# Expert results scattered to their tokens' rows, and plain loads in place of gathers

## What is computed

```python
xt = x.reshape(T, Dd)                      # T = 2048 tokens
scores = softmax(xt @ Wr.T)                # 8 experts
k_scores, k_ids = top_k(scores, 2)
k_w = k_scores / (k_scores.sum(-1) + eps)
h = relu(xt @ Wg[e].T) * (xt @ Wu[e].T)    # 512 wide
out_e = h @ Wd[e].T
out = sum over the two chosen e of k_w[e] * out_e
```

## Time and profile before

| | |
|---|---|
| median of 3 runs | 1273.29 us (1267.78 to 1274.67) |
| profiled execution | 1278.91 us, of it the span 1277.1 us |
| PE busy | 87% of the span |
| DVE, ACT, POOL busy | 71%, 63%, 44% |
| last eviction of an expert tile | 1249.10 us |

### The profile page before, as it was taken

One profiled execution on the slowest core, in us unless ns is written; L12 is line 12 of the kernel. 1 busy time (PEld: TensorE's weight loads), 2 busy tenths in 40 slices (PEclk: granted clock), 3 DMA queues, 4 the chain that ended last, 5 costly groups with the idle time before them and its releaser, 6 DMA issues.

```text
span 1277.1 us, 36892 instructions
## 1 busy us (share of the span) xinstructions
PE 1109.0 (87%) x14528; PEld 798.7 (63%) x14528; DVE 902.2 (71%) x1818; ACT 808.4 (63%) x1488; POOL 564.4 (44%) x1193
## 2 busy tenths in 40 slices
PE   5667899999999999999989989986879878798990
PEld 1123576776677676667767767775545445698990
DVE  4757689997899998899976787784457567152231
ACT  5786788887998897897876676663334333232430
POOL 1004366666566666666755664654010103104404
PEclk9989799999999999999998999998699888898995
DMA  4012262222222212222213222311001103398982
GB/s 151 1 49 69 49 164 54 56 72 53 51 65 55 58 45 78 53 54 72 54 45 83 62 54 71 66 37 30 10 14 22 28 9 125 112 295 285 335 292 54
DMA packets 131661, 106.33 MB, mean 83 GB/s; under 512 B 60112, under 2 KB 119376, under 8 KB 131232
## 3 DMA queue, kind: packets, MB, share of 16 engines
q1 hardware_dynamic: 129440, 99.76, 27.8%
q0 software_dynamic: 2048, 4.20, 1.0%
HBM read 84.06 MB, written 15.73 MB: 78 GB/s over the span
## 4 chain that ended last, share of the span: by engine, by line
PE 50%; DVE 24%; issue 10%; ACT 6%; POOL 5%; DMA 3%; SPq 2%; DVEq 0%; POOLq 0%; ACTq 0%
PE bank L1051 6%; PE pair L731 5%; DVE vc L1500 4%; DVE kc L1500 4%; PE bank L1058 3%; PE pair L695 3%; PE bank L1005 3%; DVE AM L1570 3%; PE bank L878 2%; PE bank L833 2%; PE bank L783 2%; POOL xs L1997 2%; DVE X L1654 2%; PE pair L849 2%; PE bank L772 2%
## 5 line engine op out<-in xcount | busy, mean ns | idle before, releaser
L1954 POOL TENSOR_TENSOR SU<-SU 128x14 f32<-128x14 f32 (+6 forms) x448 | 151.1, 337 | 35.1
L1950 POOL TENSOR_TENSOR SU<-SU 128x14 f32<-128x14 f32 (+6 forms) x448 | 149.6, 334 | 34.9
L1500 DVE SCALAR_TENSOR_TENSOR vc<-vy,conv,vc 128x512 f32<-128x512 f32 x192 | 152.8, 796 | 16.8 <-ACT vc L1193 16.4
L1500 DVE SCALAR_TENSOR_TENSOR kc<-ky,conv,kc 128x512 f32<-128x512 f32 x162 | 125.7, 797 | 10.0 <-ACT kc L1167 8.3
L2020 POOL TENSOR_TENSOR RR<-RR,nh 128x8 f32<-128x8 f32 x32 | 65.1, 2036 | 150.0 <-DVE RR L1642 149.9
L1836 DVE TENSOR_TENSOR vy<-bank,vc 128x512 f32<-128x512 f32 x46 | 31.8, 692 | 98.5 <-PE bank L1051 97.2
L731 PE MATMUL pair<-SM,KQ 64*128 64x128 f32 (+1 forms) x512 | 75.0, 370 | 20.3 <-DVE AM L1570 14.1
L1926 POOL TENSOR_TENSOR st<-st,nh 128x4 f32<-128x4 f32 x16 | 18.9, 1180 | 148.1 <-DVE st L1476 110.3
L695 PE MATMUL pair<-xnT,WQ 128*128 128x512 f32 x128 | 76.6, 682 | 0.2 <-DVE SM L1519 0.2
L663 PE MATMUL pair<-xnT,WQ 128*128 128x512 f32 x128 | 70.3, 634 | 5.9 <-ACT qb L1167 5.1
L1799 DVE TENSOR_REDUCE SM<-pair 128x4 f32<-128x1024 f32 x32 | 39.1, 1222 | 40.4 <-PE pair L963 40.3
(11 more groups left out here) (316 smaller groups left out, 3154.9 us busy)
## 6 DMA issues: line engine op xcount, KB each, us to landing
AM<-in_wex_dram SPq DMA_DIRECT2D x32, 768.0 KB, 5.6
SM<-dscr SPq DMA_DIRECT2D x58, 256.0 KB, 3.8
V<-in_wex_dram SPq DMA_DIRECT2D x14, 768.0 KB, 5.1
et<-dscr SPq DMA_DIRECT2D x38, 256.0 KB, 3.8
SM<-fscr SPq DMA_DIRECT2D x64, 128.0 KB, 2.9
scratch<-AM SPq DMA_DIRECT2D x128, 48.0 KB, 1.8
SU<-scratch SPq DMA_DIRECT2D x256, 15.5 KB
xs<-idle SPq DMA_DIRECT2D x2, 1472.0 KB, 9.4
```

Source lines behind the costliest of these rows:

```text
L1500: e.scalar_tensor_tensor(c, y[:, :, k:k + 256], conv[:, ct, k:k + 1], c, ALU.mult, ALU.add).then_inc(s_c, 1)
L1950: e.tensor_tensor(tmp[:, 0:k, 0:15 - k], sub[:, 0:k, k:k + 1].to_broadcast([128, k, 15 - k]), sub[:, k:k + 1, k + 1:16].to_broadcast([128, ...
L1954: e.tensor_tensor(sub[:, 0:k, k + 1:16], sub[:, 0:k, k + 1:16], tmp[:, 0:k, 0:15 - k], ALU.subtract).then_inc(s_su, 1)
```

## The change

Results no longer come back by gathers. Each sorted row now carries where its result belongs, and the results are scattered there from SBUF.

- A row of `xs` has 130 columns. Column 128 is the token's number in its half (128 h + partition), written by DVE into the normed tokens from the constant `place`; column 129 is 0 for choice 0 and 1024 for choice 1, written by a memset on POOL. So POOL scatters all eight token tiles for k = 0, waits until these have landed, sets column 129, and scatters them again for k = 1. Rows that no token fills keep 2048 and up, so that their results go to rows which nobody reads.
- `clear()` fills `xs` with these numbers and zeroes, now from a DRAM input instead of SBUF, in rows of 520 bytes.
- `place` (DVE), in each tile's tick: the sum of the two columns as an integer, into one of six index buffers.
- `back` (POOL) replaces `store`: an indirect DMA with that index writes the tile's results to `ys[S]`, now (16 + 23) x 128 rows. In the ticks in which POOL sends the scatters of half 1, the results of tiles 13 to 19 are put off to ticks 70 and 73. `YB` has six buffers instead of three, the loads six places instead of eight, and a load also waits for `place` of the tile six before it.
- `res` is on SP: per half four plain loads, two for each four token tiles (one per choice).

```diff
@@ scratch and buffers
-        xs_d = [nc.dram_tensor(f"xs{i}", (NS * 128, 128), F32, kind="Internal").ap() for i in range(2)]
-        ys_d = [nc.dram_tensor(f"ys{i}", (NS * 128, 128), F32, kind="Internal").ap() for i in range(2)]
+        xs_d = [nc.dram_tensor(f"xs{i}", (NS * 128, 130), F32, kind="Internal").ap() for i in range(2)]
+        ys_d = [nc.dram_tensor(f"ys{i}", ((16 + NS) * 128, 128), F32, kind="Internal").ap() for i in range(2)]
...
-        XSR = [kcf[:, 128 * k:128 * k + 128] for k in range(NX)]
+        XSR = [kcf[:, 130 * k:130 * k + 130] for k in range(NX)]
+        place = kyf[:, 880:888]
+        IDX = [PPf2[:, k:k + 1] for k in range(NX)]
...
-        YB = [YFf[:, 640 + 128 * k:768 + 128 * k] for k in range(3)]
+        YB = [YFf[:, 640 + 128 * k:768 + 128 * k] for k in range(3)] + [SU[:, 128 * k:128 * k + 128] for k in range(3)]
+        NY = len(YB)
@@ ticks
-            for h in range(8):
-                t = b + 5 + (2 * h // 3 if S else h)
-                at_tick(t, ("scat", S, h, t))
+            for m in range(16):
+                t = b + 5 + m // (3 if S else 2)
+                at_tick(t, ("scat", S, m, t))
...
-            at_tick(TILE[i] + 1, ("store", i))
+            at_tick(TILE[i], ("place", i))
+            at_tick({67: 70, 68: 73, 69: 73, 70: 73, 71: 73, 72: 73}.get(TILE[i] + 1, TILE[i] + 1), ("back", i))
...
-            b = TB[1] + 3 + 2 * t if t < 8 else TILE[-1] + 2 + t - 8
-            at_tick(b, ("res", t))
+            b = TB[1] + 3 + 2 * t if t < 8 else TILE[-1] + 2
+            if t % 4 == 0:
+                at_tick(b, ("res", t // 4))
@@ SP
             def clear():
-                e.wait_ge(s_set, NS_SET - 1)
-                z = idle[:, 0:256].bitcast(F32)
                 for S in range(2):
-                    e.dma_start(xs_d[S].rearrange("(i p) c -> p i c", p=128), z.unsqueeze(1).to_broadcast([128, NS, 128])).then_inc(l_zero, 16)
+                    e.dma_start(xs_d[S].rearrange("(i p) c -> p i c", p=128),
+                                lay2_d[:, LAY2 + 8:].rearrange("p (i c) -> p i c", i=NS)).then_inc(l_zero, 16)
...
                     if i >= NX:
                         e.wait_ge(s_et, i - NX + 1)
+                        e.wait_ge(s_place, i - NX + 1)
...
-                elif kind == "store":
-                    i, = a
-                    e.wait_ge(s_ye, i + 1)
-                    e.dma_start(ys_d[i // NS][128 * (i % NS):128 * (i % NS) + 128, :], YB[i % 3]).then_inc(l_ys[i % 3], 16)
+                elif kind == "res":
+                    u, = a
+                    S, half = u // 2, u % 2
+                    for k in range(NY):
+                        e.wait_ge(l_ys[k], 16 * len([i for i in range(NS * (S + 1)) if i % NY == k]))
+                    if S:
+                        e.wait_ge(s_xo, 8 * half + 8)
+                    for k in range(2):
+                        r = 1024 * k + 512 * half
+                        e.dma_start(GB[half][:, :, k, :], ys_d[S][r:r + 512, :].rearrange("(t p) n -> p t n", p=128)).then_inc(l_g[half], 16)
@@ ACT, eviction of Y
-                    if i >= 3:
-                        e.wait_ge(l_ys[i % 3], 16 * (i // 3))
-                    e.activation(YB[i % 3], bank[7][:, 0:128], ACT.Copy).then_inc(s_ye, 1)
+                    if i >= NY:
+                        e.wait_ge(l_ys[i % NY], 16 * (i // NY))
+                    e.activation(YB[i % NY], bank[7][:, 0:128], ACT.Copy).then_inc(s_ye, 1)
@@ DVE
+                elif kind == "place":
+                    i, = a
+                    e.wait_ge(l_xs[i % NX], 16 * (i // NX) + 16)
+                    if i >= NX:
+                        e.wait_ge(l_ys[(i - NX) % NY], 16 * ((i - NX) // NY) + 16)
+                    e.tensor_scalar(IDX[i % NX], XSR[i % NX][:, 128:129], XSR[i % NX][:, 129:130], None, ALU.add).then_inc(s_place, 1)
@@ POOL
                     if h == 0:
-                        e.wait_ge(l_zero, 32)
-                    for k in range(2):
-                        e.indirect_dma_start(xs_d[S], bass.IndirectOffsetOnAxis(ap=POS[S][:, k, h:h + 1], axis=0), XE[S][:, h, :],
-                                             None).then_inc(l_sc[S], 16)
-                elif kind == "res":
...
+                        if k == 0:
+                            e.wait_ge(l_zero, 32)
+                        else:
+                            e.wait_ge(l_sc[S], 128)
+                        e.memset(XE[S][:, :, 129], 1024.0 * k).then_inc(s_one, 1)
+                        e.wait_ge(s_one, 2 * S + k + 4)
+                    e.indirect_dma_start(xs_d[S], bass.IndirectOffsetOnAxis(ap=POS[S][:, k, h:h + 1], axis=0), XE[S][:, h, :],
+                                         None).then_inc(l_sc[S], 16)
+                elif kind == "back":
+                    i, = a
+                    e.wait_ge(s_ye, i + 1)
+                    e.wait_ge(s_place, i + 1)
+                    e.indirect_dma_start(ys_d[i // NS], bass.IndirectOffsetOnAxis(ap=IDX[i % NX], axis=0), YB[i % NY], None).then_inc(
+                        l_ys[i % NY], 16)
```

More of the change, by code:

```diff
@@ L25 @@
 LAY2 = 624
-NX = 8
+NX = 6
 def flat(a):
@@ L99, in program @@
         vy = sb("vy", [128, 2, 2, 259])
-        kc = sb("kc", [128, 2, 512])
+        KC = sb("kc", [128, 1040])
+        kc = KC[:, 0:1024].rearrange("p (a t) -> p a t", a=2)
         vc = sb("vc", [128, 2, 512])
-        et = sb("et", [128, 2, 512])
-        qb = sb("qb", [128, 2, 512])
+        ET = sb("et", [128, 1040])
+        et = ET[:, 0:1024].rearrange("p (a t) -> p a t", a=2)
+        QB = sb("qb", [128, 1040])
+        qb = QB[:, 0:1024].rearrange("p (a t) -> p a t", a=2)
         xT = sb("xnT", [128, 3, 512])
@@ L142, in program @@
         CT = [Uf[:, 512 * i + 256:512 * i + 512] for i in range(2)]
+        PPf2 = flat(PP[:, :, :])[:, 376:376 + NX].bitcast(U32)
         XE = [a.rearrange("p (t n) -> p t n", t=8) for a in (etf, qbf)]
-        XSR = [kcf[:, 128 * k:128 * k + 128] for k in range(NX)]
+        XSR = [kcf[:, 130 * k:130 * k + 130] for k in range(NX)]
+        place = kyf[:, 880:888]
+        IDX = [PPf2[:, k:k + 1] for k in range(NX)]
         XST = [YFf[:, 384 + 128 * k:512 + 128 * k] for k in range(2)]
-        YB = [YFf[:, 640 + 128 * k:768 + 128 * k] for k in range(3)]
+        YB = [YFf[:, 640 + 128 * k:768 + 128 * k] for k in range(3)] + [SU[:, 128 * k:128 * k + 128] for k in range(3)]
+        NY = len(YB)
         RG = [vcf[:, 512 * k:512 * k + 512] for k in range(2)]
         HB = [vyf[:, 512 * k:512 * k + 512] for k in range(2)]
-        GB = [[Vf[:, 3072 + 256 * i + 128 * k:3072 + 256 * i + 128 * k + 128] for k in range(2)] for i in range(4)]
+        GB = [a.rearrange("p (t k n) -> p t k n", t=4, k=2) for a in (Vf[:, 3072:4096], AMf[:, 8192:9216])]
         WR = [AMf[:, 1536 * k:1536 * k + 1536] for k in range(4)] + [Vf[:, 1536 * k:1536 * k + 1536] for k in range(2)]
@@ L207, in program @@
         l_sc, l_xs, l_w, l_ys, l_g = (sem("l_sc0"), sem("l_sc1")), [sem(f"l_xs{k}") for k in range(NX)], [sem(f"l_w{k}") for k in range(6)], [
-            sem(f"l_ys{k}") for k in range(3)], [sem(f"l_g{k}") for k in range(4)]
+            sem(f"l_ys{k}") for k in range(6)], [sem(f"l_g{k}") for k in range(2)]
+        s_place = sem("s_place")
         s_et, s_xt, s_g, s_u, s_rg, s_h, s_y, s_ye, s_xo = (sem(f"s_{n}") for n in ("et", "xt", "g", "u", "rg", "h", "y", "ye", "xo"))
@@ L927, in prep @@
                 if kind == "Q":
-                    e.wait_ge(l_aw, 16)
+                    e.wait_ge(l_aw, 32)
                     e.wait_ge(s_nxT, NI["at", q] + 1)
@@ L1042, in expert @@
                     e.wait_ge(*free(("T", i)))
-                    e.transpose(bank[7][:, 0:128], XSR[i % NX], ident[:, :]).then_inc(s_et, 1)
+                    e.transpose(bank[7][:, 0:128], XSR[i % NX][:, 0:128], ident[:, :]).then_inc(s_et, 1)
                 elif kind in ("G", "U"):
@@ L1820, in item @@
                     norm2(*a)
+                    key = a[0]
+                    if key[0] == "ex" and key[1] % 2 == 0:
+                        e.tensor_copy(XE[key[1] // 2][:, :, 128], place)
+                elif kind == "place":
[4 more added lines that the diff above has]
+                    e.tensor_scalar(IDX[i % NX], XSR[i % NX][:, 128:129], XSR[i % NX][:, 129:130], None, ALU.add).then_inc(s_place, 1)
                 elif kind == "signed":
@@ L1987, in item @@
                 elif kind == "scat":
-                    S, h, t = a
+                    S, m, t = a
+                    h, k = m % 8, m // 8
                     e.wait_ge(s_ix2, 2 * S + 1)
@@ L1994, in item @@
                     if h == 0:
-                        e.wait_ge(l_zero, 32)
-                    for k in range(2):
-                        e.indirect_dma_start(xs_d[S], bass.IndirectOffsetOnAxis(ap=POS[S][:, k, h:h + 1], axis=0), XE[S][:, h, :],
-                                             None).then_inc(l_sc[S], 16)
-                elif kind == "res":
```

(13 more changed lines are left out.)

17 lines of the change are left out of this document (9 added, 8 removed).

## The result

| | before | changed |
|---|---|---|
| median of 20 runs each, us | 1276.07 (1267.78 to 1281.38) | 1280.05 (1273.39 to 1288.09) |
| ratio, with its 95% interval | | 1.0036 [1.0019, 1.0054] |
| profiled execution (its span), us | 1278.9 (1277.1) | 1285.7 (1283.9) |

The changed kernel is slower by 0.36%: a small loss, but a real one, where the sum had said a small gain. The two profiled executions lie 6.8 us apart in span. To say where they went, I read the same marks in both traces: DVE's transposes of SU in round 1 and round 5, the first scatter and T(0) of half 0, the first scatter and T(23) of half 1, the last eviction, and the end.

What follows compares the result with a forecast made beforehand. PE was taken as full during expert tiles and idle before each half's first tile and in the tail; -10.1 (tail) + 5.4 (half 1) + 0.6 (half 0) + 3.0 (clearing) = -1.1 us, giving 1272.2 against 1273.3, range 1264.5 to 1281.

Steps and rivals of the forecast that it cites:

- The clearing: Early stage, SP's queue: clearing xs from DRAM in 520 B rows loses 3 us, passed on through POOL and ACT to PE.
- Upper end: Clearing of xs: each byte costs twice, 3.06 MB at 141 GB/s instead of 283, 10.9 us more.
- the lower end: Clearing of xs: it moves at the same rate as before, loss 0.
- My hope against it: Early stage: ACT also waits 3.2 us for PE in the same round, so part of a slower clearing may be caught up.
- The prediction's own sign of being wrong: Early stage: the forecast is wrong if it loses over 6 us or nothing.
- The slower rival: SP's queue, 159 to 185 us: clearing at half its rate delays ACT's exponentials, 10.9 instead of 3, total 1280.1; chance 0.20.
- The tail: After the last tile: one scatter, plain loads and eight additions replace 16 gathers, gain 10.1 us.
- my better end: Tail after the last tile: scatter landing in 2.5 us and loads in 3.2 give a gain of 12.1.
- Half 1's start: POOL's scatters before T(23): the wait for choice 0 and one result scatter make T(23) 5.4 us late.
- The second queue: Half 1's start: evictions of tiles 19 and 20 wait for delayed result scatters, end just ahead of T(23)'s load, cost nothing.
- Half 0's start: Before T(0): the wait for choice 0 falls into a hole on POOL; two memsets and some landing lose 0.6 us.
- Result buffers as a limit: Half 1, rival: result scatters landing in 8 us or more hold PE after T(23); at 9 us +3, 1275.2; chance 0.07.

Runs made afterwards that it cites:

- A: The kind of chip on which the kernel before took 1275 us; on the other kind it took 1306 to 1307.
- two groups of scatters: Changed kernel with choice 0's scatters in two groups of four, each with its own semaphore and memset: 0.9945 of before's time, on chips where before took 1306 to 1307.
- the contiguous clearing: Changed kernel with xs cleared from DRAM as one contiguous stretch of 11,960 B per partition instead of 23 rows of 520 B: 0.9932 of before's time, median 1267.42 us.

## Why the prediction was wrong

The forecast was 1272.2, a gain of 1.1 us on either base; measured were 1280.05, a loss of 4.0 between medians and 6.8 between profiles. The time lies inside the range of 1264.5 to 1281, at its upper end, and the ratio inside 0.5%, but on the other side of 1.

- **The clearing: the step that failed.** "Upper end: each byte costs twice" and "I stay near the lower end and take 3". Measured: 15.0 in the first trace, 13.9 and 14.0 in two others of the changed kernel on A; the landing 12.3 us longer. Two faults. I put the question to the wrong feature: DRAM as a source costs nothing (9.4 us), rows of 520 B do (+12.4 alone), and the earlier trace rows could speak only of rows that start on multiples of 512 B in xs. And the bound wasn't a bound: it priced the clearing's own bytes, not what the loads behind it on SP's queue lose. The decay rows came 13.7 us late, not 10.9; the rest of the 15.0, 1.3 us, is what is left for PE's restart at the granted clock of 0.50 shown above. My hope against it, that ACT's 3.2 us wait for PE would catch a part, didn't come true: PE had run out of work too and stood idle from 179 to 187 us, and the same wait is still there in the changed kernel, 3.11 us long. The prediction's own sign of being wrong, an early stage that loses over 6 us, is what came.
- **The page that spoke against me was right that the rows cost.** The Trainium skill, DMA: Bandwidth & Descriptors, How a descriptor splits into AXI transactions, charges unaligned starts with extra beats. My estimate from it, 1.3 to 1.5 times, is short of the measured 2.3 times (21.7 against 9.4 us; 1.8 times in the kernel before). It counts only bytes fetched in vain on the reading side, and by it rows of 512 B at multiples of 64 B would pay as well; those landed in 9.4 us here. So the page gave the right warning, but its reason isn't shown by these runs.
- **The slower rival is what happened**, in its place and with its mechanism: SP's queue from 159 us, the decay rows, POOL, ACT's exponentials. Its time, 1280.1, agrees with the 1280.05 by luck: it had 10.9 for 15.0, the tail gained 3.4 more than it allowed, and its base, a median of 1273.3 from three runs, was 2.8 under the 1276.07 of twenty. It should have had more than 0.20, since the only evidence for "near the lower end" was a row about other rows.
- **The tail: right in kind, too small.** 13.5 instead of 10.1 and past my better end of 12.1. The scatter landed in 2.27 us (taken: 3.8; nothing else was on the queues), the additions took 5.3 instead of 6.1 because with all data there no wait stands between them, and the end came 2.3 us after the last one instead of 3.2.
- **Half 1's start: right, with two terms off against each other.** From the eighth scatter's issue to the memset 5.8 us (taken 4.7), so the last scatter began 6.7 us later relative to the first, not 5.4. But it landed in 2.50 instead of the 5.45 of before that I had kept. Net 3.8, and 3.7 and 4.4 in the other traces on A. The second queue behaved as forecast (T(i+3) waits for the eviction of tile i, as the example of T(23) has it, not of tile i+1): T(22) waits 5.71 us for the eviction of tile 19, and T(23) in the end for its own load. With two groups of scatters the whole of it went, 26.46 again.
- **Half 0's start: 2.4 instead of 0.6.** The eighth scatter took 6.3 us from its issue to the memset behind it, above my 3.8 to 5.5, so its wait came out of the cover of the norm's pow. In the other two traces on A it is 0.1 and 0.5, so the size is one execution's.
- **Result buffers as a limit** didn't show: T(23) to the last eviction is 73.5 us in both.

Without the cost of the clearing's rows the sum would have been right in sign and too modest: the contiguous clearing gives 0.9932 and, with the groups, 0.99, some 9 and 13 us of 1275, against the -4.1 that the other three terms of the forecast add up to.

## What to carry to other kernels

Before a row gets two more words, ask what all its bulk transfers will do: widened from 512 to 520 B, a 3 MB fill went to under half its rate, while contiguous stretches or rows on multiples of 64 B kept it. A bulk transfer costs what stands behind it on its queue; cut into slices, the same rows of 520 B cost nothing measurable. And when a range hangs on one feature of a transfer, check that the row behind it varies that feature and no other.
